# An attention and routed-experts kernel: new tables of jobs by slot, and weighted sums copied by ScalarE and normalised by GpSimd

## What is computed

```python
q = x @ q_w + q_b ; k, v = x @ kv_w + kv_b          # 16 heads of 8 channels
att = q k^T / sqrt(8) + alibi bias, causal, softmax   # 512 x 512 per head
y = att @ v ; x = layernorm(x + y @ o_w + o_b)
probs = softmax(x @ gate_w.T) ; top 2 of 8 experts, their weights renormalised
x = layernorm(x + shared_ffn(x) + sum over the 2 experts of weight * ffn_e(x))
```

## Time and profile before

| | us |
|---|---|
| median of 3 runs | 1071.94 (1069.91 to 1072.63) |
| the profiled execution | 1072.98 |
| its span, from the first to the last instruction | 1071.2 |
| outside the span | 1.8 |
| busy in the span: TensorE / VectorE / ScalarE / GpSimd | 997.4 / 762.7 / 757.3 / 635.2 |

### The profile page before, as it was taken

One profiled execution on the slowest core, in us unless ns is written; L12 is line 12 of the kernel. 1 busy time (PEld: TensorE's weight loads), 2 busy tenths in 40 slices (PEclk: granted clock), 3 DMA queues, 4 the chain that ended last, 5 costly groups with the idle time before them and its releaser, 6 DMA issues. The chain is left out here.

```text
span 1071.2 us, 27623 instructions
## 1 busy us (share of the span) xinstructions
PE 997.4 (93%) x8742; PEld 666.7 (62%) x8742; DVE 762.7 (71%) x2150; ACT 757.3 (71%) x1678; POOL 635.2 (59%) x1134
## 2 busy tenths in 40 slices
PE   3999999999999979999999869999999999999992
PEld 1444444444444434444444348789999999999882
DVE  2798888888888898888989436744333335666595
ACT  2287888788878867887887744477777777888553
POOL 1155545554555555888788843667777774666442
PEclk9999999999999999999999989999999999999996
DMA  5333323323242322435231143123232223444343
GB/s 151 98 105 88 88 82 83 105 82 89 77 110 74 89 76 79 115 93 141 75 96 56 56 164 131 31 73 86 82 84 84 82 73 102 126 125 134 91 139 96
DMA packets 123485, 102.02 MB, mean 95 GB/s; under 512 B 18976, under 2 KB 113958, under 8 KB 122690
## 3 DMA queue, kind: packets, MB, share of 16 engines
q1 hardware_dynamic: 113458, 78.19, 26.6%
q0 software_dynamic: 8640, 16.87, 4.8%
q10 hardware_dynamic: 1248, 5.21, 1.3%
HBM read 39.51 MB, written 35.66 MB: 70 GB/s over the span
## 5 line engine op out<-in xcount | busy, mean ns | idle before, releaser
L769 ACT ACTIVATE probs<-scores 128x512 f32<-128x512 f32 x640 | 353.0, 598 | 47.0 <-PE scores L670 45.2
L840 POOL TENSOR_SCALAR_AFFINE_SELECT probs<-probs 128x256 f32<-128x256 f32 (+1 forms) x640 | 224.0, 364 | 162.5 <-ACT probs L769 150.1
L1271 DVE TENSOR_TENSOR e_hid<-e_gate,e_up_ps 128x352 f32<-128x352 f32 (+2 forms) x190 | 106.6, 561 | 178.8 <-ACT e_gate L1546 159.1
L670 PE MATMUL scores<-qstack,kstack 64*128 64x512 bf16 (+3 forms) x1024 | 226.5, 302 | 6.5 <-ACT probs L769 5.2
L686 PE MATMUL pv<-probs,vaug 128*32 128x512 f32 (+3 forms) x2048 | 191.4, 446 | 0.4 <-POOL probs L840 0.4
L966 DVE CUSTOM_DVE_ANT_0 summed<-maxed,last_mask 128x512 bf16<-128x512 f32 x256 | 167.0, 683 | 30.0 <-PE maxed L642 29.4
L1629 POOL DMA_INDIRECT y_tokens<-e_raw,e_row_i x142 | 140.4, 989 | 65.7 <-issue 32.0
L973 DVE TENSOR_REDUCE maxB<-maxed 128x4 f32<-128x512 f32 x256 | 163.6, 679 | 9.9 <-PE maxed L653 9.9
L670 PEld LDWEIGHTS scores<-qstack,kstack 64*128 64x128 bf16 x1024 | 64.8, 94 | 154.1 <-ACT probs L769 96.7
L1546 ACT ACTIVATE e_gate<-e_gate_ps 128x352 f32<-128x352 f32 (+2 forms) x190 | 94.5, 497 | 76.1 <-PE e_gate_ps L1443 45.4
L647 PE MATMUL maxed<-kstack,qstack 64*128 64x128 bf16 (+2 forms) x768 | 142.1, 281 | 4.6 <-DVE maxB L973 4.3
(11 more groups left out here) (193 smaller groups left out, 1721.1 us busy)
## 6 DMA issues: line engine op xcount, KB each, us to landing
qstack<-parts SPq DMA_DIRECT2D x96, 128.0 KB
kstack<-parts SPq DMA_DIRECT2D x96, 128.0 KB
x_sorted<-zeros SPq DMA_DIRECT2D x16, 580.5 KB, 5.2
e_xs<-x_sorted SPq DMA_DIRECT2D x142, 64.5 KB
e_raw<-y_tokens SPq DMA_DIRECT2D x64, 128.0 KB
xin<-in_x SPq DMA_DIRECT2D x16, 256.0 KB, 3.5
e_group_in<-x1T_all SPq DMA_DIRECT2D x16, 256.0 KB, 2.9
out<-e_raw SPq DMA_DIRECT2D x64, 64.0 KB
```

The costliest lines, as they stand in the source:

```text
L670: last = pe.matmul(scores[st.at(0, SEQ_UNITS, n) % SB][:, col:col + width], ks[rows, slot, kt * P:(kt + 1) * P], q[rows, slot, kt * P:T], ...
L769: act.activation(probs[g % 2][:, u * T:(u + 1) * T], scores[st.at(0, SEQ_UNITS, UNITS * g + u) % SB][:], ACT.Exp).then_inc(S["exp_done"], 1)
L840: pool.affine_select(out=view, in_=view, compare_op=ALU.is_ge, fill=0.0, base=0, pattern=pattern, channel_multiplier=-1).then_inc(S["maske ...
L1271: dve.tensor_tensor(hid[step % len(hid)][rows, 0:cols], gate[step % 2][rows, 0:cols], up_ps[step % 2][rows, 0:cols], ALU.mult).then_inc(S[ ...
```

## The change

The tables of jobs are others, for all four engines. The normalising is split in three: ScalarE copies the 9 useful columns of each head (8 weighted sums and their softmax sum) of every `y` bank to SBUF, VectorE takes the reciprocals of two banks at a time from there (`ia`, `ib`), and GpSimd multiplies two banks at a time. The reader that frees `misc` after a `y` is the copy. The copied sums share their memory (`tokens`) with the tokens `x1_tiles` that job `o` writes later.

```diff
--- before.py
+++ after.py
@@ -178,14 +178,14 @@
 DIAGONAL = (None, slice(0, 4, 3), slice(1, 4, 2))
 MAX_AT = (30, 0, 10, 20)
 PLACES = {
-    "PE": {0: "xt", 1: "pv0", 3: "q", 4: "pv1", 6: "pv2", 7: "k", 8: "pv3", 10: "y0", 12: "pv0 mb", 13: "pv1 y1", 14: "pv2",
-        16: "y2", 17: "pv3 y3", 19: "v", 20: "pv0 yn", 23: "o vo", 24: "pv1", 25: "pv2 rt", 26: "pv3", 30: "pv0", 32: "ma",
-        33: "pv1", 34: "pv2", 35: "x1t", 36: "pv3", 37: "lg"},
-    "ACT": {0: "xt", 3: "q", 7: "k", 8: "keep", 11: "mb", 13: "mrb qr", 14: "kr", 16: "keep", 19: "v", 20: "yn", 25: "keep",
-        28: "ln0", 29: "ln1", 30: "ln2", 31: "ma", 33: "mra ln3", 35: "x1t", 37: "keep"},
-    "POOL": {10: "res", 11: "qr", 15: "kr", 23: "rstd"},
-    "DVE": {4: "qs", 8: "ks", 10: "y0", 11: "mb", 13: "mrb y1", 15: "y2", 16: "y3", 23: "o", 24: "vo", 25: "rt", 31: "ma",
-        33: "mra", 37: "lg"},
+    "PE": {0: "xt pv0", 3: "q", 6: "pv1 pv2", 7: "k", 8: "pv3", 10: "y0", 12: "mb pv0", 14: "y1 pv1 pv2", 15: "y2",
+        17: "pv3 y3", 19: "v", 21: "pv0 yn", 22: "vo", 24: "o", 25: "pv1 pv2 pv3", 30: "rt", 31: "pv0", 33: "ma pv1",
+        34: "pv2", 36: "x1t", 37: "pv3 lg"},
+    "ACT": {0: "xt", 3: "q", 7: "k", 8: "keep", 10: "y0", 12: "mb mrb qr", 13: "y1", 14: "kr", 15: "y2", 16: "keep y3",
+        20: "v", 21: "yn", 25: "keep", 28: "ln0 ln1", 30: "ln2", 31: "ma", 33: "mra ln3", 35: "x1t", 36: "keep"},
+    "POOL": {6: "res", 12: "qr", 14: "ia", 15: "kr ib", 23: "rstd"},
+    "DVE": {4: "qs", 8: "ks", 11: "mb", 12: "mrb", 13: "ia", 16: "ib", 24: "o", 25: "vo", 29: "rt", 32: "ma", 33: "mra",
+        37: "lg"},
 }
 
 
@@ -212,11 +212,11 @@
 READERS = {
     "rt": ("placed", 0, 1), "vo": ("vb_moved", 0, 1),
     "xt": ("xT_ready", 1, 1), "q": ("qk_split", 2, 1), "k": ("qk_split", 2, 2),
-    "y0": ("y_normed", 8, 2), "y1": ("y_normed", 8, 4), "y2": ("y_normed", 8, 6), "y3": ("y_normed", 8, 8),
+    "y0": ("y_copied", 4, 1), "y1": ("y_copied", 4, 2), "y2": ("y_copied", 4, 3), "y3": ("y_copied", 4, 4),
     "v": ("v_ready", 1, 1), "yn": ("ynT_ready", 1, 1), "o": ("z_ready", 1, 1), "x1t": ("x1T_ready", 1, 1),
     "ma": ("m_rest", 4, 1), "mb": ("m_rest", 4, 3), "lg": ("logits_kept", 1, 1),
 }
-STAGE = {"xt": 2, "q": 2, "k": 2, "qs": 2, "ks": 2, "qr": 2, "kr": 2, "v": 1, "ma": 1, "mra": 1, "mb": 0, "mrb": 0, "yn": -1, "o": -1, "ln0": -1, "ln1": -1, "ln2": -1, "ln3": -1, "x1t": -1, "lg": -1,
+STAGE = {"xt": 2, "q": 2, "k": 2, "qs": 2, "ks": 2, "qr": 2, "kr": 2, "v": 1, "ma": 1, "mra": 1, "mb": 0, "mrb": 0, "yn": -1, "o": -1, "ln0": -1, "ln1": -1, "ln2": -1, "ln3": -1, "x1t": -1, "lg": -1, "ia": -1, "ib": -1,
          "rt": 0, "vo": 0, "y0": -1, "y1": -1, "y2": -1, "y3": -1}
 
 
@@ -412,7 +412,7 @@
         rowmax = sb("rowmax", [P, NH, QT])
         mparts = sb("mparts", [HALF_HEADS * QT, PARTS, P], BF16)
         mrest = sb("mrest", [HALF_HEADS * QT, P])
-        rsum = sb("rsum", [P, NH])
+        inverse = sb("inverse", [P, QT * NH])
         ynorm = sb("ynorm", [P, QT, NH, HD])
         ynT = sb("ynT", [P, T])
         xres = sb("xres", [P, QT, C])
@@ -424,7 +424,9 @@
         shift = sb("shift", [P, QT])
         minus_half = sb("minus_half", [P, QT])
         eps = sb("eps", [P, QT])
-        x1_tiles = sb("x1_tiles", [P, QT, C])
+        tokens = sb("tokens", [P, QT * NH * (HD + 1)])
+        ysum = tokens[:].rearrange("p (n d) -> p n d", d=HD + 1)
+        x1_tiles = tokens[:, 0:QT * C].rearrange("p (i c) -> p i c", c=C)
         x1T = ynT
 
         scores = [ps(f"scores{n}") for n in range(SB)]
@@ -434,7 +436,7 @@
 
         names = """const_loaded masks_loaded late_loaded stack_rows_loaded0 stack_rows_loaded1 stack_rows_loaded2 const_ready unit_ready max_ready pv_ready xT_ps q_ps k_ps v_ps m_ps y_ps ynT_ps o_ps
             x1T_ps lg_ps exp_done xT_ready qk_high qk_mid y_kept m_high ynT_ready x1T_ready max_taken rowmax_ready
-            qk_split m_rest v_ready y_normed z_ready ln_done rstd_ready logits_kept vaug_zeroed rows_zeroed masked qk_low res_biased x1_done x_loaded0 x_loaded1 wait_passed
+            qk_split m_rest v_ready y_normed z_ready ln_done rstd_ready logits_kept vaug_zeroed rows_zeroed masked qk_low res_biased x1_done x_loaded0 x_loaded1 y_copied y_inverse wait_passed
             xres_loaded max_rows routed chosen prefix_ps placed places x_scattered ids_set routing_set vb_moved vo_ps x1T_stored shared_loaded""".split()
         S = {n: sem(n) for n in names}
         x_loaded = [S["x_loaded0"], S["x_loaded1"]]
@@ -589,7 +591,7 @@
                             pe.wait_ge(S["y_kept"], st.at(-1, 4, 4))
                         transposes([yraw[st.par(-1)][:, g, i * P:(i + 1) * P] for g in range(NQUAD)], "y_ps")
                     elif name == "yn":
-                        pe.wait_ge(S["y_normed"], st.at(-1, 8, 8))
+                        pe.wait_ge(S["y_normed"], st.at(-1, 2, 2))
                         transposes([ynorm[:, i].rearrange("p h d -> p (h d)") for i in range(QT)], "ynT_ps")
                     elif name == "o":
                         pe.wait_ge(S["ynT_ready"], st.at(-1, 1, 1))
@@ -742,6 +744,12 @@
                         half = "ab".index(name[2])
                         act.wait_ge(S["m_rest"], st.at(1 - half, 4, 2 * half + 1))
                         copy(mparts[:, 1, :], mrest[:], "m_high")
+                    elif name[0] == "y" and name[1] != "n":
+                        i = int(name[1])
+                        act.wait_ge(S["y_ps"], st.at(-1, 4, i + 1))
+                        if i == 0 and not st.first(-1):
+                            act.wait_ge(S["y_normed"], st.at(-2, 2, 2))
+                        copy(ysum[:, i * NH:(i + 1) * NH, :], misc[:].rearrange("p (h c) -> p h c", c=VW)[:, :, 0:HD + 1], "y_copied")
                     elif name == "yn":
                         act.wait_ge(S["ynT_ps"], st.at(-1, 1, 1))
                         if not st.first(-1):
@@ -858,6 +866,15 @@
                                                    ALU.pow).then_inc(S["rstd_ready"], 1)
                                 pool.wait_ge(S["rstd_ready"], st.at(-1, 4, 3))
                                 pool.tensor_tensor(shift[:], minus_mean[:], rstd[:], ALU.mult).then_inc(S["rstd_ready"], 1)
+                            elif item in ("ia", "ib") and st.chained():
+                                k = "ab".index(item[1])
+                                half = slice(k * 2 * NH, (k + 1) * 2 * NH)
+                                pool.wait_ge(S["y_inverse"], st.at(-1, 2, k + 1))
+                                if k == 0 and not st.first(-1):
+                                    pool.wait_ge(S["ynT_ps"], st.at(-2, 1, 1))
+                                pool.tensor_tensor(ynorm[:, 2 * k:2 * k + 2].rearrange("p i h d -> p (i h) d"), ysum[:, half, 0:HD],
+                                                   inverse[:, half].unsqueeze(2).to_broadcast([P, 2 * NH, HD]),
+                                                   ALU.mult).then_inc(S["y_normed"], 1)
                             elif item == "res" and st.chained():
                                 pool.wait_ge(S["xres_loaded"], st.at(-1, 16, 16))
                                 if st.first(-1):
@@ -904,25 +921,19 @@
                         dve.wait_ge(S["m_rest"], st.at(1 - half, 4, 2 * half + 1))
                         dve.tensor_tensor(mparts[:, 2, :], mrest[:], mparts[:, 1, :],
                                           ALU.subtract).then_inc(S["m_rest"], 1)
-                    elif name[0] == "y" and name[1] != "n":
-
-                        i = int(name[1])
-                        dve.wait_ge(S["y_ps"], st.at(-1, 4, i + 1))
-                        if i == 0 and not st.first(-1):
-                            dve.wait_ge(S["ynT_ps"], st.at(-2, 1, 1))
-                        if i or not st.first(-1):
-                            dve.wait_ge(S["y_normed"], st.at(-1, 8, 2 * i))
-                        view = misc[:].rearrange("p (h c) -> p h c", c=VW)
-                        dve.reciprocal(rsum[:].unsqueeze(2), view[:, :, HD:HD + 1]).then_inc(S["y_normed"], 1)
-                        dve.wait_ge(S["y_normed"], st.at(-1, 8, 2 * i + 1))
-                        dve.tensor_tensor(ynorm[:, i], view[:, :, 0:HD], rsum[:].unsqueeze(2).to_broadcast([P, NH, HD]),
-                                          ALU.mult).then_inc(S["y_normed"], 1)
+                    elif name in ("ia", "ib"):
+                        k = "ab".index(name[1])
+                        half = slice(k * 2 * NH, (k + 1) * 2 * NH)
+                        dve.wait_ge(S["y_copied"], st.at(-1, 4, 2 * k + 2))
+                        if k == 0 and not st.first(-1):
+                            dve.wait_ge(S["y_normed"], st.at(-2, 2, 2))
+                        dve.reciprocal(inverse[:, half].unsqueeze(2), ysum[:, half, HD:HD + 1]).then_inc(S["y_inverse"], 1)
                     elif name == "o":
                         dve.wait_ge(S["o_ps"], st.at(-1, 1, 1))
```

(2 more changed lines are left out.)

## The result

The changed kernel took 1059.28 us (median; 1056.98 to 1062.73), the kernel before, run beside it, 1072.11 (1069.91 to 1072.63). The ratio is 0.9887, with a 95% interval of 0.9856 to 0.9918: faster by 1.1%. The profiled execution took 1059.75 us with a span of 1058.0, against a span of 1071.2 before. Those 13.2 us are what the traces must account for.

What follows compares the result with a forecast made beforehand. TensorE's own program was taken to bound the step. 0.68 + 0.28 - 0.12 + 0.19 = 1.03 us a step, 12.4 for twelve steps, 12.9 with step 0, gave 1059 us; forecast 1053 to 1066, range 1046 to 1073.

Steps and rivals of the forecast that it cites:

- The stretch ahead of `pv0`: From yn to the pv0 ahead of slot 32: VectorE's reductions around job o set its length, so gain 0.
- the chain of the forecast: Behind o, the last slot's maxima wait for VectorE's fourth reduction to free a bank; pv0 begins 0.05 + 0.32 us later.
- Merged runs: Rest of the step: 21 TensorE slot runs become 16, saving 3 x 0.10 + 2 x 0.19 = 0.68 us.
- `pv` behind `pv`: Slots 6 and 14: two joins of weighted-sum jobs on TensorE save 0.14 us each, 0.28 a step.
- `mb`, 0.12 lost: TensorE's mb moves from behind pv0 to behind a run: 0.33 us instead of 0.21, so 0.12 lost.
- `x1t`'s wait: x1t moves from slot 35 to 36, so TensorE's 0.19 us wait for ScalarE's last layer norm goes.
- VectorE's relief: VectorE is relieved of 1.6 us, counted at nothing because that work does not stand where VectorE is late.
- ScalarE's copies, covered: Four new copies of 0.28 us a step; slots behind y0 and y2 cover the wait, so 0 lost.
- the rival at 1088: ScalarE's copies uncovered at slots 10, 13, 15, 16: 0.60 us each, step 1.4 longer, 1088 us; chance 0.09.
- `ib`'s chain: Ahead of yn: copy 0.28, reciprocal 0.3, GpSimd product 0.75 us, covered by TensorE's work with over 0.5 to spare.
- GpSimd and VectorE: Rival: they block each other; mrb and mra each take 0.82 us more, step 0.6 longer, 1079 us; chance 0.04.
- Step 9, 0: The routing step: 1.0 us lost as rt follows the wait behind o, against 1.03 saved, so 0.

Runs made afterwards that it cites:

- split_inside: Changed kernel with the block pv1 pv2 pv3 taken apart into slots 25, 26 and 27, between yn and pv0: 1060.24 us, 0.9900 of the kernel before.
- offload_only: Kernel before with its own TensorE order and only the normalisation moved to ScalarE copies, VectorE reciprocals and GpSimd products: 1072.68 us, ratio 1.0000.
- tables_only: Kernel before with the new job tables, the normalisation left on VectorE: 1074.32 us, ratio 1.0017.
- rt_spread: Changed kernel with step 9's routing cut up: TensorE's rt at slot 26, VectorE's eight groups in pairs behind slots 26 to 29; 1056.94 us.
- joins_b: rt_spread with y2 joined behind pv2 (slot 14), pv2 joined to ma pv1 (slot 33), and VectorE's ks one slot earlier: 1052.22 us.
- v_28: Changed kernel with job v moved from slot 19 to slot 28, between yn and pv0: 1065.64 us, 0.9936 of the kernel before.
- split_outside: Changed kernel with two joins taken apart: pv0 one slot behind xt, pv1 two slots ahead of pv2; 1062.59 us, 0.9909 of the kernel before.

## Why the prediction was right, and where not

The time, 1059 forecast and 1059.28 measured, came from steps that were in part wrong in opposite directions: the step was to gain 1.03 us and gained 1.24 (steps 1 to 8 and everything from step 10 to the last `lg` gave 14.9, not 12.4), and step 9 and the experts gave 2.5 us back. That the two nearly cancel is luck.

- **The stretch ahead of `pv0`, 0.** Right: 7.03 against 7.04, by the chain of the forecast, and `split_inside` shows that TensorE's order there costs nothing.
- **Merged runs, 0.68.** Measured 0.57: three that ended on a 512 slot gave 0.10, 0.11 and 0.11, as priced; of the two on a 384 + 128 slot one gave 0.20 and the other, made into a run of three, 0.05. The price 0.19 was taken from a second slot and used for a third, which costs 0.31 and there 0.08 more by the wait for VectorE's reduction. The run of slots 18 and 19 got 0.07 shorter besides.
- **`pv` behind `pv`, 0.28.** Right: 0.14 at each of the two.
- **`mb`, 0.12 lost.** Nothing was lost: `mb pv0` takes 1.21 us, as `pv0 mb` did. A `pv` behind the single transpose of `mb` or `ma` saves 0.11 to 0.12 again; behind four transposes (`xt`, `y1`) it saves 0.01 or less. I had set all four to nothing, so `ma pv1` gave 0.12 unforeseen (0.21 for `ma`, 177.21 to 177.42, against 0.33 in the earlier trace rows).
- **`x1t`'s wait, 0.19.** Gone; the run ahead of it was 0.26 longer than its like, so this much.
- Together 0.57 + 0.07 + 0.28 + 0.12 + 0.26 = 1.30, less 0.06 by which `yn` and `x1t` behind other work took longer: the 1.24.
- **VectorE's relief, "counted at nothing, since where it is late (behind `o`) these do not stand".** This is the step that failed in its reason. In the old order it is worth nothing, as `offload_only` shows. In the new order it is a condition: with VectorE still emptying the bank, 1.06 us of the 1.24 go back, most of it to the wait at `mb`; or, with `mb` behind `pv0`, 0.64 and 0.50, of which 0.54 and 0.40 are waits at `y2` and behind it. I priced the new tables with the bank always free in time and had the reason for that, ScalarE's copy, only as a cost.
- **ScalarE's copies, covered.** Right: no job of TensorE waits for one of them in the step shown, and the rival at 1088 fell. (Its 0.60 a copy was the time of 512 columns; one of these takes 0.29.) `ib`'s chain is in time for `yn`.
- **GpSimd and VectorE.** Nothing of that rival is seen: `mrb` and `mra` took 0.294 us (median) and 0.424 at most, against 0.275 and 1.091 in the earlier trace rows. The long row does not go with the products. It began at 600.29, while GpSimd's sum `res` ran from 599.88 for 1.27; `offload_only`, with the products and with `res` still behind slot 10, shows 1.101 beside the same sum, and `tables_only`, without the products and with `res` behind slot 6, 0.416 at most. The change has `res` behind slot 6. None of these subtractions in the change is more than 0.15 us longer than the median before (0.424 - 0.275), where the rival needed 0.82. The Trainium skill (SBUF — State Buffer, section Who interferes with whom) has VectorE instructions with both inputs in SBUF exclude GpSimd's reads of it. The two long rows agree with that.
- **Step 9, 0.** Wrong: 0.83 lost beside the 1.24 it should have gained, 2.07 in all. The 1.0 that I set against the gain at the routing was 0.27 (from `y1` on step 9 is 6.85 us longer than a full step, before 6.58). The other 1.80 lie ahead of `y1`, where I had put nothing: VectorE is late there with the routing's earlier operations, the merged run of slots 4 to 6 waits for it, and behind the wait at `y0` TensorE runs at the lower clock, which it did not before (mean of the step 0.89, before 0.92).
- **Start-up and the experts.** Step 0 gained nothing (0.5 forecast); the 0.8 were won ahead of it. The experts' start shows the clock at 0.50 and 0.51 from 615 to 625 us, before only from 630 to 635 (0.50). That the 1.7 us come from it is not shown; and they are no fixed price of the change, since with the same experts that part took 451.6 us in the traces of `split_inside` and `rt_spread`, 453.6 in that of `joins_b` and 454.0 in that of `v_28`. Nor did I test why over 40 to 50 us the clock was 0.56 in the change and 1.00 before.

## What to carry to other kernels

An order can be tightened only as far as whoever empties the shared buffer is quick: price a new order together with the queue of its reader, and when a change has two halves, run each alone, since here 0 and 0.2 us a step (0.7 in a better order) made 1.24. A job that fills another engine's wait is free where it stands; before it is moved into a wait, look at what its old place turns into.

## What the runs showed of the hardware that was not expected

- One transpose of 128 columns takes 0.33 us between two runs of slots and 0.20 to 0.22 next to a `pv`, ahead of it or behind it (`ma` and `mb`, before and after; in one step of `split_outside` `mb` took 0.31 ahead of `pv0`); four transposes take 0.58 or 0.59 in either place.
- A third 384 + 128 slot in a run costs TensorE 0.31 us where it need not wait (`joins_b`, slots 15 to 17) and 0.39 at slot 6 of the change, where it waits for a bank; a second costs 0.23. With 512 columns both cost 0.21 to 0.22.
- After idle times of 0.92 and 1.82 us within three us the granted clock was 0.65 and 0.67 over the ten us around them, on the mean the same as after one of 3.95 us (0.58 and 0.74).
- In step 9 of the change an idle time of 1.46 us ahead of `y0`, some five us after one of 0.32, was followed by three us at 0.50. In the kernel before one of 1.47 us at the same job was followed by 1.00, as was one of 0.53 in `joins_b`. What decides between them these runs do not show.
